# VectorE's and GpSimd's small work moved to other steps, gates of two batches computed after the last expert tile, rows sent in steps 0 to 7 of the next iteration

## The reference

```
x = layernorm(x + softmax(mask(Q K^T / sqrt(8))) V @ Wo + bo)
xn = layernorm(x) * gamma + beta
combine, idx = top2(softmax(xn @ Wg.T))
out = layernorm(x + sum_k combine[k] * expert_{idx[k]}(xn))
```

## Time and profile before

| | |
|---|---|
| median of 3 runs | 1069.77 us (1069.46 to 1071.54) |
| profiled execution | 1072.32 us |
| its span in the profile | 1070.4 us |
| TensorE's mean granted clock | 0.945 of 2.4 GHz |
| attention iterations | about 42 us each, to 698 us of the span |
| expert tiles | about 710 to 1040 us |
| last batches | 1040 to 1070 us |

### The profile page before, as it was taken

One profiled execution on the slowest core, in us unless ns is written; L12 is line 12 of the kernel. 1 busy time (PEld: TensorE's weight loads), 2 busy tenths in 40 slices (PEclk: granted clock), 3 DMA queues, 4 the chain that ended last, 5 costly groups with the idle time before them and its releaser, 6 DMA issues.

```text
span 1070.4 us, 29495 instructions
## 1 busy us (share of the span) xinstructions
PE 904.4 (84%) x9185; PEld 578.7 (54%) x9185; DVE 777.7 (73%) x1970; ACT 686.5 (64%) x1402; POOL 686.4 (64%) x1018
## 2 busy tenths in 40 slices
PE   5788889889898898898888988869899989998740
PEld 2334444444444444444444444349899879997740
DVE  2887788888888888878888888945455464477645
ACT  1476677667677676776776766736766645566543
POOL 6343557586686776856857757738667456568774
PEclk9899999899899899999989989989999999999985
DMA  7533563553544534434344322333223222265515
GB/s 210 183 124 90 160 174 94 164 150 107 180 121 136 180 93 140 150 83 155 103 130 156 106 90 70 104 88 99 69 64 92 66 80 78 70 229 184 157 48 177
DMA packets 169384, 132.54 MB, mean 124 GB/s; under 512 B 52939, under 2 KB 155378, under 8 KB 169105
## 3 DMA queue, kind: packets, MB, share of 16 engines
q1 hardware_dynamic: 156880, 112.48, 35.5%
q0 software_dynamic: 8704, 17.06, 4.8%
q10 hardware_dynamic: 3648, 1.12, 0.5%
HBM read 71.55 MB, written 61.15 MB: 124 GB/s over the span
## 4 chain that ended last, share of the span: by engine, by line
PE 52%; DVE 26%; issue 8%; POOL 7%; ACT 4%; DMA 2%; ACTq 0%; SPq 0%; DVEq 0%; POOLq 0%
DVE negmax L1235 13%; PE ring L1204 9%; PE ring L1188 9%; PE ps_v L1124 9%; PE ring L1061 5%; PE ring L1092 5%; PE ring L1107 3%; POOL y_d L674 2%; DVE mhl L1252 2%; DVE rt L1306 2%; PE ps_m L938 2%; PE ps_m L960 2%; ACT probs L769 2%; PE ps_m L949 2%; PE ps_m L954 1%
## 5 line engine op out<-in xcount | busy, mean ns | idle before, releaser
L1235 DVE TENSOR_REDUCE negmax<-ring 128x2 f32<-128x1024 f32 (+3 forms) x512 | 406.7, 815 | 67.5 <-PE ring L1107 63.5
L769 ACT ACTIVATE probs<-ring 128x768 f32<-128x768 f32 (+1 forms) x384 | 336.5, 880 | 154.7 <-PE ring L1061 148.5
L637 POOL TENSOR_SCALAR_AFFINE_SELECT probs<-probs 128x512 f32<-128x512 f32 x256 | 163.5, 641 | 196.1 <-ACT probs L769 192.6
L887 ACT ACTIVATE vpad<-ring,b_s 128x128 f32<-128x128 f32 x576 | 164.4, 369 | 101.7 <-PE ring L1188 101.4
L674 POOL DMA_INDIRECT y_d<-vpad,xs x144 | 146.6, 1018 | 108.5 <-DVE vpad L1519 78.1
L1124 PE MATMUL ps_v<-probs,vpad 128*32 128x512 f32 (+3 forms) x2048 | 194.0, 466 | 6.7 <-POOL probs L637 6.7
L1204 PE MATMUL ring<-qarea,vpad 128*128 x1152 | 157.0, 279 | 20.0 <-ACT vpad L887 19.7
L1188 PE MATMUL ring<-vpad,w_t 128*128 128x128 f32 x1152 | 156.9, 280 | 9.3 <-issue 8.9
L1204 PEld LDWEIGHTS ring<-qarea,vpad 128*128 128x128 f32 x1152 | 140.6, 192 | 25.9 <-issue 24.0
L1188 PEld LDWEIGHTS ring<-vpad,w_t 128*128 128x128 f32 x1152 | 142.3, 194 | 13.6 <-issue 13.3
L651 POOL DMA_INDIRECT rows_d<-xn,slot x128 | 129.4, 1011 | 25.8 <-issue 24.9
(11 more groups left out here) (181 smaller groups left out, 1230.8 us busy)
## 6 DMA issues: line engine op xcount, KB each, us to landing
kside<-qk_d SPq DMA_DIRECT2D x32, 512.0 KB, 6.5
qk_d<-qarea SPq DMA_DIRECT2D x32, 384.0 KB, 2.7
xs<-rows_d SPq DMA_DIRECT2D x144, 66.0 KB, 1.9
qk_d<-qarea SPq DMA_DIRECT2D x32, 256.0 KB, 2.4
qarea<-qk_d SPq DMA_DIRECT2D x16, 512.0 KB, 6.8
qodd<-qk_d SPq DMA_DIRECT2D x16, 512.0 KB, 7.2
probs<-y_d SPq DMA_DIRECT2D x16, 512.0 KB, 5.0
xin<-L_attn_x SPq DMA_DIRECT2D x16, 256.0 KB, 3.2
```

What stands on the lines that cost most here:

```text
L637: pool.affine_select(out=diag, in_=diag, pattern=[[0, 4], [1, P]], compare_op=ALU.is_ge, fill=0.0, base=0, channel_multiplier=-1).then_inc ...
L769: nc.scalar.activation(of_unit(h // 2, part), ring[:, 2 * part % 3, :, (0, P, P)[part]:S], ACT.Exp, scale=SCALE).then_inc(sem("exp_done"), 1)
L887: ins = nc.scalar.activation(ht[:, n % 4, c, :], ps_a[:, n % 4, c * P:(c + 1) * P], ACT.Gelu_apprx_tanh, bias=b1_s[:, bass.ds(e, 1), c:c + ...
L1235: ins = nc.vector.tensor_reduce(negmax[:, n // 6 % 2, qb, s:s + 2], ring[:, (2 * n + 1) % 3, :, c0:c0 + nk], AX.X, ALU.max, negate=True)
```

## The change

- `make_rows` stands at steps 6, 8, 9 instead of 7, 8, 9, and its second part also waits until the rows of the batch two before have all been read by their DMAs (`rows_sent`).
- The eight row DMAs of a batch stand at steps 0 to 7 of the next iteration (batch i-4 there) instead of steps 6 to 13. In iteration 16 both batch 12 (steps 0 to 7) and batch 13 (steps 8 to 15) are sent, and 14 and 15 at steps 8 to 15 of iterations 17 and 18.
- The residual sum is made in place in `xin`, which has four buffers now, at step 10 instead of 13; `xbo` is gone. The load of x waits for the residual sum of an earlier batch.
- VectorE: routing operations 0 and 1 stay at half-steps 26 and 27, 2 to 14 stand at half-steps 0 to 12 of the next iteration, 15 and 16 at 13, 17 at 14, `rows_of` at 15. The rank product goes from step 4 to step 6 (`RK_STEP`), the second gate exponential from step 1 to 3.
- The gates of batches 14 and 15 (`LATE` = 2): three copies keep the exponents; ScalarE takes the exponentials in two instructions after the last tile, and VectorE makes the gates in three (`late_gates`).
- `result` uses the register that `weights` loaded for the same tile instead of loading it once more.
- In iteration 16, `divide` of batch 15 stands ahead of the ranks at half-step 13, the rank product waits for it, and `aT` instead of `uT` waits for the routing. The second `plan_part` starts at half-step 16 instead of 12, `pad_ends` at step 10 instead of 9.

```diff
-        xin = sb("xin", [P, 2, QB, D])
-        xbo = sb("xbo", [P, 2, QB, D])
+        xin = sb("xin", [P, 4, QB, D])
...
-        LG_STEP, RK_STEP = 12, 4
+        LG_STEP, RK_STEP = 12, 6
...
-            need(sp, sem("xbo_ready"), 1, i, 1, sem("sp_passed"))
-            need(sp, ready("xT"), 1, i, 1, sem("sp_passed"))
-            sp.dma_start(xin[:, b.parity], x_rows[bass.ds(b.value * S, S), :].rearrange(
+            need(sp, freed("wo"), 1, b, -3, sem("sp_passed"))
+            sp.dma_start(xin[:, b.value % 4], x_rows[bass.ds(b.value * S, S), :].rearrange(
...
-                    if rb.exists(NB) and 7 <= h <= 9:
-                        make_rows(pool, rb, h - 7)
-                    if late.exists(NB) and 6 <= h <= 13:
-
-                        q, k = (h - 6) // 2, (h - 6) % 2
-                        if h == 6:
-                            need(pool, sem("rows_sent"), 16 * TOPK * QB, late, 0, sem("pool_passed"))
-                            need(pool, sem("slot_ready"), 1, late, 1, sem("pool_passed"))
-                            need(pool, sem("xn_ready"), 1, late, 1, sem("pool_passed"))
-                        pool.indirect_dma_start(
-                            rows_d, bass.IndirectOffsetOnAxis(ap=slot[:, late.parity, k, q:q + 1], axis=0),
-                            xn[:, late.parity, q, k, :], None).then_inc(sem("rows_sent"), 16)
-                    if nxt.exists(NB) and h == 13:
...
+                    if rb.exists(NB) and h in (6, 8, 9):
+                        make_rows(pool, rb, (6, 8, 9).index(h))
+                    if h < 8 and i.value <= NB:
+                        send_rows(i.plus(-4), h)
+                    if h >= 8 and i.value >= NB:
+                        send_rows(late, h - 8)
+                    if nxt.exists(NB) and h == 10:
+
+                        need(pool, ready("xT"), 1, nxt, 1, sem("pool_passed"))
...
+                        pool.tensor_tensor(x_of, x_of, across(bo_b[:], QB), ALU.add).then_inc(sem("xbo_ready"), 1)
...
                     need(pool, ready("nT"), 1, b.plus(-1), 0, sem("pool_passed"))
+                    need(pool, sem("rows_sent"), 16 * TOPK * QB, b, -16 * TOPK * QB, sem("pool_passed"))
                     pool.tensor_copy(xn[:, b.parity, :, :, D].bitcast(I32), dest[:]).then_inc(sem("xn_steps"), 1)
...
-                    if h == 15:
+                    if h == 15 and rb.exists(NB - LATE):
...
-                if h == 1 and i.plus(-3).exists(NB):
+                if h == 3 and i.plus(-3).exists(NB - LATE):
...
+                if n == NT:
+                    act.wait_ge(sem("route"), ROUTE * NB)
+                    nc.scalar.activation(late_terms[:, :, :, 0:E], late_diff[:], ACT.Exp, bias=tiny[:, :]).then_inc(
+                        sem("late_exp"), 1)
+                    nc.scalar.activation(late_terms[:, :, :, E], late_best[:], ACT.Exp).then_inc(sem("late_exp"), 1)
...
-                        pe.wait_ge(freed("uT"), 2 * NB - 1)
+                        pe.wait_ge(freed("uT"), 2 * NB)
...
+            def keep_exponents(k, part):
+                if part == 2:
+                    return V.tensor_copy(late_best[:, k], d_best)
+                half = slice(2 * part, 2 * part + 2)
+                return V.tensor_copy(late_diff[:, k, half], diff[:, half])
+
+            def late_gates():
+                dve.wait_ge(sem("late_exp"), 2)
+                V.tensor_reduce(late_sum[:], late_terms[:], AX.X, ALU.add).then_inc(sem("late_gates"), 1)
...
+                if 12 <= n < 15 and not b.exists(NB - LATE):
+                    keep_exponents(b.value - (NB - LATE), n - 12).then_inc(sem("route"), 1)
+                    return
...
-                        if at >= 26:
+                        if at in (26, 27):
                             route(rb, at - 26)
-                        if at < 9:
-                            route(late, 6 + at)
-                        if at == 10:
+                        if at < 13:
+                            route(late, 2 + at)
+                        if at == 14:
                             route(late, 17)
-                        if at == 11:
+                        if at == 15:
                             rows_of(late)
...
             def weights(n):
-                e = expert_of(n)
+                e = experts[n] = expert_of(n)
...
             def result(n):
-                e = expert_of(n)
+                e = experts.pop(n)
...
+                if n == NT + 2:
+                    late_gates()
```

More of the change, by code:

```diff
@@ L90, in build_program @@
     ROUTE = 18
+    LATE = 2
     RING = 12
@@ L165, in build_program @@
         rv = sb("rv", [P, 8, QB])
+        late_diff = sb("late_diff", [P, LATE, QB, E])
+        late_best = sb("late_best", [P, LATE, QB])
+        late_terms = sb("late_terms", [P, LATE, QB, E + 2])
+        late_sum = sb("late_sum", [P, LATE, QB])
         onehot = sb("onehot", [P, QB + 1, E], BF16)
@@ L183, in build_program @@
         b1_r = sb("b1_r", [E * FC, P])
-        b2_b = xin[:, :, :, :].rearrange("p a q d -> p (a q) d")
+        b2_b = xin[:, 0:2].rearrange("p a q d -> p (a q) d")
         xs = sb("xs", [P, RING, ROW])
@@ L513, in body @@
                             load_attention(sp, i.plus(-1))
-                        if h == 9 and i.value == NB + 2:
+                        if h == 10 and i.value == NB + 2:
                             pad_ends(1)
@@ L626, in _ @@
             pool.memset(terms[:], 1.0)
+            pool.memset(late_terms[:], 1.0)
             pool.memset(tiny[:], math.log(1e-9))
@@ L668, in body, with send_rows @@
                         send(n - 1)
+            def send_rows(b, n):
+                if not b.exists(NB):
+                    return
+                q, k = n // 2, n % 2
+                if n == 0:
+                    need(pool, sem("rows_sent"), 16 * TOPK * QB, b, 0, sem("pool_passed"))
+                    need(pool, sem("slot_ready"), 1, b, 1, sem("pool_passed"))
+                    need(pool, sem("xn_ready"), 1, b, 1, sem("pool_passed"))
+                pool.indirect_dma_start(
+                    rows_d, bass.IndirectOffsetOnAxis(ap=slot[:, b.parity, k, q:q + 1], axis=0),
+                    xn[:, b.parity, q, k, :], None).then_inc(sem("rows_sent"), 16)
             def send(n):
@@ L930, in misc @@
                         break
-                if not i.loop and i.value >= NB and (name, i.value) in (("uT", NB), ("nT", NB + 1)):
+                if not i.loop and i.value >= NB and (name, i.value) in (("aT", NB), ("nT", NB + 1)):
                     pe.wait_ge(sem("route"), ROUTE * (i.value - 3) + 17)
@@ L1329, in _ @@
             assert len(ROUTING) == ROUTE
+            def keep_exponents(k, part):
[6 more added lines that the diff above has]
+                V.tensor_reduce(late_sum[:], late_terms[:], AX.X, ALU.add).then_inc(sem("late_gates"), 1)
+                of = slice((NB - LATE) * QB, NB * QB)
+                dve.wait_ge(sem("late_gates"), 1)
+                V.reciprocal(gates[:, of, 0], late_sum[:].rearrange("p k q -> p (k q)")).then_inc(sem("late_gates"), 1)
+                dve.wait_ge(sem("late_gates"), 2)
+                V.tensor_tensor(gates[:, of, 1], late_terms[:, :, :, E].rearrange("p k q -> p (k q)"), gates[:, of, 0],
+                                ALU.mult).then_inc(sem("late_gates"), 1)
             def route(b, n):
@@ L1378, in body @@
                                 "p (q e) -> p q e", e=E)).then_inc(freed("lg"), 1)
+                        if at == 13 and prev.exists(NB) and i.value == NB:
+                            divide(prev, 1, False)
+                            divide(prev, 1, True)
                         if at == 2 * RK_STEP + 1:
@@ L1405, in body @@
                         if prev.exists(NB):
-                            if at == 13:
+                            if at == 13 and i.value < NB:
                                 divide(prev, 1, False)
@@ L1413, in body @@
                                 V.tensor_tensor(ysum[:], ps_m[:].rearrange("p (q d) -> p q d", q=QB),
-                                                xbo[:, prev.parity], ALU.add).then_inc(freed("wo"), 1)
+                                                xin[:, prev.value % 4], ALU.add).then_inc(freed("wo"), 1)
                             if at == 26:
@@ L1424, in body @@
                             plan_part(0, at - 18)
-                        if not i.loop and i.value == NB + 2 and 12 <= at < 14 + E:
-                            if at == 12:
+                        if not i.loop and i.value == NB + 2 and 16 <= at < 18 + E:
+                            if at == 16:
                                 last_segment()
-                            plan_part(1, at - 12)
+                            plan_part(1, at - 16)
                         for n in expert_steps(i, h)[half:half + 1]:
@@ L1537, in add_choice @@
                         dve.wait_ge(sem("route"), ROUTE * NB)
+                    if b == NB - LATE:
```

(1 more changed line is left out.)

16 lines of the change are left out of this document (7 added, 9 removed).

## The result

The changed kernel takes 1065.86 us (1058.49 to 1076.03, 20 runs), the kernel before beside it 1068.80 (1062.59 to 1073.12, 20 runs). The ratio is 0.9965, 95% interval 0.995 to 0.998: faster, by 4 us and not by 22. One of its 20 runs (1076.03) was in the chip's slower state and is not in the ratio. The profiled execution has a span of 1066.1 us (before 1070.4) and a mean granted clock of 0.958 (0.945).

What follows compares the result with a forecast made beforehand. Attention iterations were taken as bound by TensorE and VectorE in turn, VectorE partly waiting for GpSimd; expert tiles by TensorE. Terms -11.4 - 4 - 7 = -22.4 gave 1047 us against 1069.8, range 1020 to 1066.

Steps and rivals of the forecast that it cites:

- landing of the eighth row DMA: Ahead of L710 on GpSimd: the DMA starts near 431.0, lands after 2.4 us at 433.4, so 0.7 us more wait.
- First stretch: 402.0 to 410.2 us of an attention iteration, VectorE full: L1306's stall and moved operations go, gain 3.8 us per iteration.
- collisions: Moved VectorE operations at half-steps 0 to 6 meet masks and row DMAs: 0.3 us lost per iteration, bounds 0 and 0.8.
- clock: TensorE's 3.1 us idle before nT brings the lower clock, counted at half its price: 0.8 us per iteration, bounds 0 and 2.0.
- Second stretch: 421.8 to 431.0 us of an iteration, VectorE full: more GpSimd work and a new wait delay nT, loss 1.75 us.
- The sum per iteration: All attention terms together, -3.8 + 1.75 + 0.8 + 0.3 = -0.95 us; over twelve iterations -11.4.
- Early iterations: Iterations 2 and 3, no rows sent at steps 0 to 7: nT doesn't wait, 2 times 2.0 us gained, -4.
- Expert tiles: Eight table loads and a register load per tile go, against small costs in iteration 16 and late gates: -7 us.
- Rival (b): Attention gives everything back: low clock after every nT wait, only 0 to 3 us plus tiles' 7 remain, 1060; 18 in 100.
- Rival (a): nT doesn't wait because GpSimd keeps up; 4.8 us gained per iteration, 1001 us; 7 in 100.
- Rival (c): Slower: rows land late beside the store's DMAs; forecast turns at a landing of 4.3 us, 1088 at 5.8; 6 in 100.
- L1306's stall: VectorE's 32-element L1306 held 1.81 us beside GpSimd's sum; priced at 3.1 us per iteration, 1.7 stall and the rest clock.

Runs made afterwards that it cites:

- e4: The kernel before with only the late gates of batches 14 and 15 and one register load less per tile; ratio to the kernel before 0.9949.
- e6: The changed kernel without the late gates and with result's register load per tile back, so only the new order remains; ratio to the kernel before 1.0066.
- c_after: The changed kernel itself, unaltered, measured again beside other runs on one chip; ratio to the kernel before 0.999.
- e1: The changed kernel with four buffers of xn instead of two, so make_rows needs only rows of four batches back; ratio to the kernel before 0.9766.
- e5: The changed kernel with row DMAs at steps 9 (one), 11 (two), then 1 (two), 2 (one), 3 (two) of the next iteration; 1017.28 us, ratio to before 0.9524.
- e8: The kernel before with only the residual sum moved to step 10, in place in four buffers of xin; ratio to the kernel before 0.9827.
- e9: The kernel before with row DMAs at steps 9, 11 and the next iteration's 1, 2, 3, and the wait for them; sum at step 13; ratio 0.9647.

## Why the prediction came out as it did

The direction came out right, the size wrong: -22.4 forecast for the profiled execution, about -4 measured. The sign owes something to luck, for it is the expert tiles' gain that makes it: the attention, which was to give 15 us, lost 2 to 7. What failed is the term for the landing of the eighth row DMA in the second stretch. It was put at 0.7 us of waiting and is 2.0 in the ten iterations; over the twelve it is 21.7 us instead of 8.4, which is 13.3 of the 18.1 us by which the forecast was off. Point by point, per iteration where it is one.

- **First stretch (-3.8) with collisions (+0.3) and clock (+0.8), -2.7 in all: right in sum.** From one L725 to the next the iteration shown takes 42.56 us (393.94 to 436.50) against 42.31; the stretch to `nT` grew by 3.25, so the rest gave 3.0, at the full clock. L1306's hold went from 1.81 to 0.2 us. In seven of the ten iterations the clock fell behind `nT` (a mean of 0.96), in three with much the same wait it did not (1.00): a bit over the half that I had put in. Those at 1.00 take 42.2 to 42.6 us, six of the others 43.3 to 44.2, so one fall costs 0.8 to 2.0 us. The mean of 0.97 over the ten is about 1.2 us of 43 and not 0.8 (an estimate).
- **Second stretch (+1.75): the step that failed, at its last term.** The count of GpSimd's work held to 0.1 us. "0.7 more" for the landing took the tile scatters' median of 2.4 us for a transfer that flies beside the attention's store. It lands after 3.36 to 3.70 us in nine of iterations 4 to 13 (4.13 once), and after 2.38 and 2.33 in 14 and 15. In the iteration shown the wait is 2.18 instead of 0.7, which makes the +1.75 into the +3.25 measured. Over the twelve waits it is 1.81. The bound of 2.6 for the stretch was too low as well. The earlier trace rows had landings up to 5.8, and I used them for a rival and not for the term. SyncE's queue in the trace of before shows the store, at the very time for which I forecast the row DMA (431.0):

```profile
430.65 0.36 SPq L416 DMA_DIRECT2D att_d<-attt  x1
```

- **The sum per iteration** would have been -0.95 + 1.3 = +0.35 with the mean wait of 2.0, and +0.47 was measured. Over ten iterations this is +4.7 instead of -9.5. The worst case of my range did not follow from my bounds: -3.0 + 2.6 + 2.0 + 0.8 is +2.4 per iteration, and I wrote +0.1.
- **Early iterations (-4):** -2.6 to the third mark; the batches before the waits run in 40 us. **Startup (0):** +2.3 in this trace. There is a wait for weights that I had counted as nothing, but by the other kernels' first marks its price is not shown.
- **Expert tiles (-7): right.** -6.5 in the trace, -5.6 by e4, 7 to 8 by e6 against c_after. All eight table loads went and one came, as forecast.
- **Rival (b), everything given back in the attention, came nearest,** by the wait's length more than by the clock; but it still had 0 to 3 us from the attention. Rival (a) had its chance in the wrong place: it is not `make_rows` keeping up with this order but another order. With the wait removed (e1) the gain is 2.3%; with the row DMAs moved clear (e5) an iteration is 3.9 us shorter, where (a) counted 4.8.
- **Rival (c) had the mechanism.** Its turning point, a landing of 4.3 us, was near: at 3.5 the attention's order already costs more than it gives (e6: 1.0066). It had no room for the tiles' 7 us.
- What I called worth 3.1 us, L1306's stall, has no price of its own. Moving the sum alone gives 1.6 us per iteration (e8), since the block goes to another operation; leaving it and moving the row DMAs gives 3.3 (e9), most of it clock. The fixed price came from two windows that differed in more than L1306: the early one sends no rows ahead of its start either, and it starts at 149.70, just after the sum of that iteration (148.13 to 149.40) had held another operation, L1304. So it was free of the sum's block by the place of the cut:

```profile
148.39 1.06 DVE L1304 TENSOR_TENSOR rt<-lg,rv 128x32 f32<-128x32 f32 x1
```

- That L1306 was held "even while only the row DMA ran" doesn't hold in general: later in the kernel before, at 751.28, it runs wholly beside a row DMA (750.70 to 751.67) and takes 0.18 us. L1304 at 402.49 does take 0.38 us beside one (401.83 to 402.84). Where a row DMA alone costs such an operation anything, it is 0.2 us here, and not the 1.7 of the sum.

The Trainium skill, "SBUF — State Buffer", section "Who interferes with whom", has the engine that issues first keep the shared pair of ports for its whole instruction, while the other waits. The lengths agree: 1.66 us for a cast of 0.2 in e8, 1.07 for a two-input operation of 0.2 in e9 (at 424.02), each ending just after a 512-element sum of 1.27. The order agrees in e9, where the sum starts first; in e8 the cast starts 0.3 us before the sum, while a row DMA is still running (427.91 to 428.88), and waits all the same.

## What to carry to other kernels

- A new wait on a DMA's completion is priced by what else the DMA engines carry at that moment: read the issuing queue's timeline around it, and take the landing from a row with such company, not a median from another stage.
- Before work is moved to another step, list the idle times of its engine ahead of the instruction that others wait for, and place the pieces into these. With the rest of the change the same, the eight row DMAs gave +0.7%, -0.8% or -4.8% against the kernel before by their place.
- A block between two engines moves with the order, and its price with the place: find out which operation it will meet next, and read the granted clock behind each place where TensorE stands still.

## What the runs showed of the hardware

- A scatter of 128 rows lands after 3.4 to 3.7 us (once 4.13) beside a store of 2048 runs of 128 bytes issued 0.2 us later, after 2.3 to 2.4 where that store is issued 1.0 to 1.3 us later, and after 2.6 beside the same bytes in 128 runs issued 0.2 us later. The store itself takes 3.3 and 2.0 us.
- The granted clock turned on little: two kernels whose TensorE stood still for 1.6 and 1.8 us at the same place had 1.00 and 0.62 in the next 4.5 us, and in the changed kernel it fell behind seven of ten waits of about the same length.
- The same kernel before took 1106.8 us on one chip and 1068 to 1070 on the others. By e4's trace the stretch with the expert tiles makes most of the difference, and no run here tells why.
